# A decoder layer on one core: the last steps of the last batch in another order, without idle products

## The reference

```python
# 1. self attention without weights; probabilities under 0.01 are split off
probs  = softmax(x @ x.T / 16)
sparse = where(probs < 0.01, 0, probs);  sparse /= sparse.sum() + 1e-9
x = layernorm(x + sparse @ x + 0.01 * broadcast(vacuum_sum) @ W.T)
# 2. cross attention: 16 heads of 16, 375 keys of the context, masked
q, k, v = x @ Wq + bq, ctx @ Wk + bk, ctx @ Wv + bv
x = layernorm(x + softmax(masked(q @ k.T / 4)) @ v @ Wo + bo)
# 3. 8 linear experts, the best 2 of each token, weighted by the router
p = softmax(x @ Wr);  top 2 of p
x = layernorm(x + sum over the top 2 of p_e * (x @ Wi[e] @ Wo[e]))
```

## Time and profile before

| | us |
|---|---|
| median of 3 runs | 748.14 |
| lowest and highest | 746.77, 750.72 |
| profiled execution, its time | 752.42 |
| profiled execution, its span | 750.6 |
| PE busy in the span | 724.8 (97%) |
| DVE busy | 662.9 (88%) |
| ACT busy | 588.6 (78%) |
| POOL busy | 213.5 (28%) |
| mean granted clock of TensorE | 0.992 |

### The profile page before, as it was taken

The page is one execution under the profiler, slowest core; times in us unless marked ns, Lnnn a source line. Parts: engine busy times, 40 slices in busy tenths (PEclk is TensorE's granted clock), DMA queues, the critical chain, the costliest instruction groups (busy, mean ns, idle before and its releaser), DMA issues.

```text
span 750.6 us, 21145 instructions
## 1 busy us (share of the span) xinstructions
PE 724.8 (97%) x7250; PEld 653.6 (87%) x7250; DVE 662.9 (88%) x2608; ACT 588.6 (78%) x1435; POOL 213.5 (28%) x384
## 2 busy tenths in 40 slices
PE   5889999999999999999999999999999999999996
PEld 4678899999999989999999989999999989889875
DVE  5587889999999889999999989999999989998976
ACT  2378989888888898888888898888988898778730
POOL 7131322133333231333331233333313333341001
PEclk9999999999999999999999999999999999999989
DMA  8865664556655565555555566556545665554100
GB/s 242 245 171 150 190 167 123 152 146 161 163 134 160 142 167 150 146 154 147 156 149 139 152 170 164 142 153 154 142 139 147 163 167 164 133 164 126 29 16 28
DMA packets 75660, 110.84 MB, mean 148 GB/s; under 512 B 14225, under 2 KB 59169, under 8 KB 75553
## 3 DMA queue, kind: packets, MB, share of 16 engines
q1 hardware_dynamic: 75552, 109.49, 54.2%
HBM read 50.23 MB, written 18.35 MB: 91 GB/s over the span
## 4 chain that ended last, share of the span: by engine, by line
PE 88%; SPq 4%; DMA 3%; DVE 3%; ACT 1%; issue 1%; POOL 0%; POOLq 0%; DVEq 0%; ACTq 0%
PE psum L1623 20%; PE psum L1397 12%; PE psum L1431 11%; PE psum L1415 10%; PE psum L1502 4%; PE psum L1490 4%; PE psum L1477 4%; PE psum L1572 3%; PE psum L1535 3%; PE psum L1513 3%; PE psum L1524 3%; SPq L393 2%; PE psum L1553 2%; PE psum L1452 2%; PE psum L1441 2%; DMA k_stack<-k_hi 1%
## 5 line engine op out<-in xcount | busy, mean ns | idle before, releaser
L934 DVE CUSTOM_DVE_ANT_0 scores_left<-psum,mask_add 112x375 f32<-112x375 f32 x512 | 270.5, 542 | 24.6 <-PE psum L1397 17.9
L613 ACT ACTIVATE probsT<-psum 125x448 f32<-125x448 f32 x384 | 201.7, 537 | 17.8 <-PE psum L1415 14.1
L598 ACT ACTIVATE psum<-mask_u 125x448 f32<-125x448 uint8 x372 | 198.2, 541 | 3.7
L1397 PE MATMUL psum<-k_stack,q_stack 96*112 96x376 f32 x512 | 183.1, 365 | 2.6 <-DMA k_stack<-k_hi 1.2
L1415 PE MATMUL psum<-q_stack,k_stack 97*125 97x224 f32 x768 | 148.2, 280 | 2.3 <-ACT psum L598 1.1
L1415 PEld LDWEIGHTS psum<-q_stack,k_stack 97*125 97x125 f32 x768 | 134.7, 188 | 13.1 <-ACT psum L598 2.5
L1166 DVE SCALAR_TENSOR_TENSOR late<-psum,gate,late 128x256 f32<-128x256 f32 x224 | 107.8, 481 | 21.0 <-PE psum L1623 12.3
L562 POOL TENSOR_TENSOR ctx_lo<-ctx_sb,ctx_hi 128x188 fp32r<-128x188 f32 x128 | 71.5, 590 | 126.4 <-ACT ctx_hi L721 126.3
L1397 PEld LDWEIGHTS psum<-k_stack,q_stack 96*112 96x112 f32 x512 | 89.1, 177 | 13.0 <-issue 6.3
L1623 PE MATMUL psum<-we_hi,x_hi 128*128 128x512 f32 x224 | 92.0, 411 | 0.5 <-DVE gate_nmax L1111 0.5
L1623 PE MATMUL psum<-we_hi,x_lo 128*128 128x512 f32 x224 | 89.0, 397 | 0.0
(11 more groups left out here) (169 smaller groups left out, 1622.3 us busy)
## 6 DMA issues: line engine op xcount, KB each, us to landing
k_stack<-k_hi SPq DMA_DIRECT2D x256, 94.0 KB, 2.6
q_stack<-q_scratch SPq DMA_DIRECT2D x96, 224.0 KB, 3.8
ctx_sb<-in_context_T SPq DMA_DIRECT2D x32, 376.0 KB, 3.7
k_stack<-k_lo SPq DMA_DIRECT2D x128, 94.0 KB, 2.5
q_scratch<-q_hi SPq DMA_DIRECT2D x32, 224.0 KB, 2.1
q_scratch<-q_lo SPq DMA_DIRECT2D x32, 224.0 KB, 2.0
xT<-in_x_T SPq DMA_DIRECT2D x32, 112.0 KB, 2.4
x_sb<-in_x SPq DMA_DIRECT2D x32, 112.0 KB, 2.9
```

The source lines that it names most:

```text
L598: nc.scalar.activation(psum[0:KP, ST_BANKS[i % 2], 0:4 * TOK].rearrange("p (h q) -> p h q", h=4), mask_u8[b % MASKS][:, KEYS + t * TOK:KEY ...
L613: nc.scalar.activation(probsT[:, place, i % KT, :], psum[0:KP, ST_BANKS[i % 2], 0:4 * TOK], ACT.Exp, scale=-1.0).then_inc(probs_ready, 1)
L934: nc.vector.tensor_tensor_reduce(scores_left[:, n % 2, :], psum[0:TOK, S_BANKS[n % 2], 0:KEYS], mask_add[b % 2][:, :], 1.0, 3.0e38, ALU.ad ...
L1397: nc.tensor.matmul(psum[0:TOK, S_BANKS[n % 2], 0:KEYS_EVEN], q_stack[s][0:96, pair, odd, c, :], k_stack[s][0:96, pair, c, :], start=True, ...
```

## The change

Six edits, all at the end of the engines' lists:

1. PE: block pairs 6 and 7 stand ahead of `m3(25)`, 8 and 9 ahead of `weigh_values(31, 0)`, 10 and 11 ahead of `x2T_(30)`.
2. PE: `lg(26)` stands behind `weigh_values(31, 1)`, which waits for the last exponent, and no longer ahead of it. On ACT `x2_hi(30)` stands behind the last exponent and `gate_exp(26)` behind `o_sb(31)`.
3. PE: `m0(26)` is cut into two halves of three products, with `aT(31)` between them.
4. PE: `Wo(31)` stands ahead of `m1(26)`, and `x2T_(31)` ahead of `m3(26)`.
5. The ten idle products are gone, and `m1(27)` stands ahead of `m0(27)`.
6. DVE: `attn_rest(31)` stands ahead of `expert(26, 0)`; `y2(31)`, `stats2`, `mom2` stand two experts earlier, `normalize_x2(31)` two earlier and `x2_lo(31)` two earlier.

```diff
--- before.py
+++ after.py
@@ -854,7 +854,7 @@
             lay_mask(30, 11); exponent(30, 10); exponent(30, 11); v2(31); gate_exp(25); o_sb(30)
             exponent(31, 0); exponent(31, 1); exponent(31, 2); attnT(30); exponent(31, 3); nmaxT1(31)
             exponent(31, 4); exponent(31, 5); exponent(31, 6); exponent(31, 7); exponent(31, 8)
-            exponent(31, 9); x2_hi(30); exponent(31, 10); exponent(31, 11); gate_exp(26); o_sb(31); attnT(31)
+            exponent(31, 9); exponent(31, 10); exponent(31, 11); x2_hi(30); o_sb(31); gate_exp(26); attnT(31)
             x2_hi(31); gate_exp(27)
 
         @block.vector
@@ -1329,8 +1329,8 @@
             lay_last(31, 10); lay_last(31, 11); x2_lo(30); expert(25, 6); cross(26); expert(25, 7)
             gate_max(26); stats3(25); mom3(25); gate_r(26); gate_p(26); top_p(26); top_i(26)
             normalize_out(25); rden(31); o_norm(31); top_f(26); gate_a(26); gate_b(26); gate(26)
-            expert(26, 0); attn_rest(31); expert(26, 1); expert(26, 2); expert(26, 3); y2(31); stats2(31)
-            mom2(31); expert(26, 4); expert(26, 5); normalize_x2(31); expert(26, 6); expert(26, 7); x2_lo(31)
+            attn_rest(31); expert(26, 0); expert(26, 1); y2(31); stats2(31); mom2(31); expert(26, 2)
+            expert(26, 3); normalize_x2(31); expert(26, 4); expert(26, 5); x2_lo(31); expert(26, 6); expert(26, 7)
             stats3(26); cross(27); gate_max(27); mom3(26); gate_r(27); gate_p(27); top_p(27); top_i(27)
             top_f(27); gate_a(27); gate_b(27); normalize_out(26); gate(27); expert(27, 0); expert(27, 1)
             expert(27, 2); expert(27, 3); expert(27, 4); expert(27, 5); expert(27, 6); expert(27, 7)
@@ -1585,16 +1585,7 @@
                                               start=(c == 0), stop=(c == DC - 1))
                 mm.then_inc(products_done, 1)
 
-            def run_idle(count):
-
-                pe.wait_ge(max_ready, HEADS * BATCH)
-                for _ in range(count):
-                    nc.tensor.matmul(psum[:, S_BANKS[0], 0:DIM * 2], we_hi[:, 0, 0:128], we_hi[:, 0, 0:DIM * 2],
-                                     start=True, stop=True, skip_group_check=True)
-
             def lg(t):
-                if t == TILES - 1:
-                    run_idle(5)
                 if t == 0:
                     pe.wait_ge(setup_dve, 5)
                 free("lg", batch_of(t))
@@ -1608,21 +1599,22 @@
                                           start=False, stop=(c == DC - 1), skip_group_check=True)
                 mm.then_inc(done["lg"], 1)
 
-            def mix_experts(t, name):
+            def mix_experts(t, name, first=0, last=3 * DC):
 
                 if (t, name) == LAST_MIX:
                     pe.wait_ge(probs_ready, BLOCKS * BATCH)
-                else:
+                elif first == 0:
                     free(name, batch_of(t))
                 in_ring = slice(t % RING_TILES * ROWS, (t % RING_TILES + 1) * ROWS)
                 hi, lo = x2_high[:, :, in_ring], x2_low[:, :, in_ring]
                 n, width = int(name[1]), 2 * DIM
                 w_hi, w_lo = [w[:, :, n * width:(n + 1) * width] for w in (we_hi, we_lo)]
                 parts = [(c, x_part, w_part) for c in range(DC) for x_part, w_part in ((hi, w_hi), (hi, w_lo), (lo, w_hi))]
-                for n, (c, x_part, w_part) in enumerate(parts):
+                for n, (c, x_part, w_part) in list(enumerate(parts))[first:last]:
                     mm = nc.tensor.matmul(mix_bank(t, name)[0:ROWS, 0:width], x_part[:, c, :], w_part[:, c, :],
                                           start=(n == 0), stop=(n == len(parts) - 1))
-                mm.then_inc(done[name], 1)
+                if last == len(parts):
+                    mm.then_inc(done[name], 1)
 
             def m0(t):
                 if t == 0:
@@ -1768,11 +1760,12 @@
             score_block(30, 10); scores(31, 10); scores(31, 11); lg(25); scores(31, 12); score_block(30, 11)
             V2(31); scores(31, 13); weigh_values(30, 1); scores(31, 14); score_block(31, 0)
             score_block(31, 1); scores(31, 15); oT(30); m0(25); score_block(31, 2); aT(30); score_block(31, 3)
-            mx1(31); m1(25); Wo(30); score_block(31, 4); score_block(31, 5); m2(25); m3(25)
-            score_block(31, 6); score_block(31, 7); weigh_values(31, 0); score_block(31, 8)
-            score_block(31, 9); x2T_(30); score_block(31, 10); score_block(31, 11); lg(26)
-            weigh_values(31, 1); oT(31); m0(26); aT(31); m1(26); Wo(31); m2(26); m3(26); x2T_(31); run_idle(5); lg(27)
-            m0(27); m1(27); m2(27); m3(27)
+            mx1(31); m1(25); Wo(30); score_block(31, 4); score_block(31, 5); m2(25)
+            score_block(31, 6); score_block(31, 7); m3(25); score_block(31, 8); score_block(31, 9)
+            weigh_values(31, 0); score_block(31, 10); score_block(31, 11); x2T_(30)
+            weigh_values(31, 1); lg(26); oT(31)
+            mix_experts(26, "m0", 0, 3); aT(31); mix_experts(26, "m0", 3, 6); Wo(31); m1(26); m2(26)
+            x2T_(31); m3(26); lg(27); m1(27); m0(27); m2(27); m3(27)
 
 _INS = [("x", "x"), ("ctx_1024", "context_T"), ("mask_Bx1xSxS2_bk1", "mask"), ("L0_attn_W", "attn_w_T"),
         ("L0_xattn_Wq", "wq"), ("L0_xattn_bq", "bq"), ("L0_xattn_Wk", "wk"), ("L0_xattn_bk", "bk"),
```

## The result

| | before | after |
|---|---|---|
| median of 8 runs, us | 749.89 | 753.92 |
| lowest and highest | 746.77, 752.0 | 752.23, 757.65 |
| ratio, 95% interval | | 1.0066 [1.0045, 1.0087] |
| profiled execution, its time | 752.42 | 757.65 |
| its span, mean granted clock | 750.6, 0.992 | 755.9, 0.984 |

The changed kernel is slower by 0.66% by the ratio, some 5 us; the medians are 4.0 us apart. The forecast was 749.9 (range 746.5 to 752.9), a difference too small to be told from none. It was wrong: the median lies 1.0 us above the range.

A forecast was written before the change was run, and what follows sets the result against it. The tail was taken as bound by DVE's chain behind cross(27), with PE's clock and order ahead of it. The order gave -0.2 us at the profiled clock; typical executions 750.5 and 752.3 gave 748.14 + 1.8 = 749.9 us, range 746.5 to 752.9.

The forecast's parts named there:

- the new wait that the router makes: DVE: late lg(26) delays cross(26) and normalize_out(25), so rden(31) starts at 729.1 us and not 727.38.
- the 1.5 that were to show it: Sign on PE: idle 1.5 us or more ahead of aT(31) would show the forecast was right.
- The walk: Step-by-step reckoning of the tail's start times; at full clock the old order goes from 752.4 to 749.5 us.
- 751.2 against 752.2 and 753.0: New order's whole time: full clock; the profiled execution's clock; clock falling in the wait ahead of aT(31).
- the clock falls in the wait ahead of `aT(31)`: PE's wait of about 2 us there was expected to lose the full clock in nearly every execution, giving 753.0 us.
- One sign: Sign on PE: lg(27) over 1 us earlier, with cross(27) over 0.8 us behind its end.
- Blocks and values: Score blocks and first weighing, up to exponents 10 and 11: cost +0.1 us, bounded by 0 and +0.3; moving m3(25) free.
- From y2 to the router: Tail from y2(31) to lg(27): x2T at 735.3, x2_lo ends 736.8, lg(27) at 736.9, 1.4 us earlier.
- The walk for the full clock: Same reckoning at full clock: old order 749.5 us, new 751.2 with cross(27) at 737.65; gains 2.9 and 1.0.
- Rival 1: Full clock stays in the new kernel: 751.2 on the profile's scale, +0.7, so 748.8 us; chance 0.12.
- Rival 2: Router of tile 26 doesn't hold rden(31); cross(27) comes 1.6 to 1.8 us earlier, 746.3 us; chance 0.13.
- Rival 3: Clock falls late, half in the last stage: +2.5 to +3.1, some 753 us; chance 0.20 with other late falls.

The follow-up runs named there:

- e2: Changed kernel with the transpose x2T of batch 31 in another PSUM bank, free since the last scores; ratio 1.0034 to before.
- e6: Changed kernel with all of edit 1 (order of blocks, m3(25), first weighing, x2T_(30)) undone; ratio 1.0045 to before.
- e9: Kernel before with four more idle products in PE's waits, two ahead of blocks 10 and 11, two ahead of oT(31); ratio 0.9994 to before.
- e7: Changed kernel with ten idle products in PE's waits: three ahead of block 11, one ahead of the second weighing, six ahead of aT(31); ratio 1.0034 to before.
- e1: Changed kernel with weigh_values(31, 0) put back ahead of blocks 8 and 9; ratio 1.0061 to before.
- e10: Changed kernel with blocks, values and router of tile 26 as before and x2T(31) in its own PSUM bank; ratio 0.9983 to before.
- e4: Kernel before without the ten idle products, nothing else changed; ratio 1.0000 to before.
- e8: Changed kernel; blocks, values, router as before; x2T(31), lg(27) in own banks, lg(27) behind five m3(26) products; cross(27), gate_max(27) ahead of experts (26, 6), (26, 7); ratio 0.9993 to before.
- e12: Same kernel as e8 plus four idle products, two ahead of blocks 10 and 11, two ahead of oT(31); ratio 0.9980 to before.

## Why the prediction was wrong

Right were that `cross(27)` decides, since both kernels take 11.8 us from there, and the new wait that the router makes. `rden(31)` stood behind `normalize_out(25)` (731.90, released by DVE's own order). PE waited 1.00 us ahead of `aT(31)` at half clock, not the 1.5 that were to show it; in e2 and e6, at full clock up to there, it waited 1.67. The walk said that a full clock is worth 2.9 us to the old order; e9 against the profile shows 2.7. To the new order it gave 1.0 to 1.8 (751.2 against 752.2 and 753.0); e7 shows 2.6. Over the 104 executions of before beside the experiments those with a mean granted clock of 0.994 or more took 748.5 us on average (42 of them), those of 0.989 or less 751.3 (36), but this mean counts the whole span, the start too. That the clock falls in the wait ahead of `aT(31)` was so in the profiles of e2 and e6; in that of the changed kernel it fell earlier, at 727.5, behind the waits of the blocks. One sign came out against the forecast: `lg(27)` was to be over 1 us earlier and was 2.3 later (26.72 against 24.40). `Wo(31)`, put 0.67 earlier, was 0.57 later (18.66 against 18.09).

Two steps of the sum failed.

1. *Blocks and values* was put at +0.1 us, with +0.3 as its bound. It cost 1.10 (10.87 against 9.77). Two waits were put at nothing. The larger, 0.74 us, is in the words "`m3(25)` moving behind blocks 6 and 7 is free": the walk asked when DVE reads `m3(25)`, and not what PE would do without it. Block 7 had to wait for its mask, PE stood idle for 0.45 us, and `m3(25)` and the first weighing came behind that instead of filling it (e1). The smaller, 0.36 us, is the ring: `exponent(31, 9)` writes the place of `probsT` that the first weighing reads. Before, that weighing ran ahead of block 8, and the wait never showed in a row.

2. *From y2 to the router* had `x2T(31)` directly behind `normalize_x2(31)`, 2.65 us after `y2`. It was 4.92 in the profile, where expert (26, 2) also waited 1.21 us for `m1(26)` at half clock, and 3.97 at full clock. `x2T`, `m2`, `lg` and `m0` share a PSUM bank, so `x2T(31)` waits until `expert(26, 5)` has read `m2(26)`. Before, both experts ran in the POOL wait ahead of `normalize_x2(31)`; the change put them behind it. The bank was named for `m2(26)` and `m0(27)` in the description, and not asked about for the step that moved. It cost 1.15 us (y2 to x2T 3.97, with its own bank 2.82).

The sum of the order at full clock, `cross(27)` of e7 against e9, 25.72 - 22.14 = 3.58 us:

| step | us | from |
|---|---|---|
| blocks and values | +1.10 | exponent 11: 10.87 against 9.77 |
| router behind the weighing | +1.79 | y2, e7 against e10: 2.89, less 1.10 |
| aT between halves, Wo ahead of m1 | -0.91 | y2, e10 against e9 |
| bank of x2T(31) | +1.15 | y2 to x2T: 3.97 against 2.82 |
| experts (26, 2) and (26, 3) ahead of normalize_x2 | +0.27 | y2 to x2T: 2.82 against 2.55 |
| x2T to cross(27) | +0.18 | 3.27 against 3.09 |

The first two rows assume that the 1.10 us of the blocks reach `y2` whole; their sum, 2.89, is measured. The walk for the full clock had put the whole at 1.7 us (737.65 against 738.82 - 2.9 = 735.9). It was 1.0 short at blocks and values and 1.3 short from `y2` to `cross(27)`; the router with `aT` and `Wo` it had put 0.4 too high (1.3 against 1.79 - 0.91 = 0.88). The timed ratio adds to the 3.6 us of the order some 1.4 us, which fits a clock that is lower on average (0.989 over the 8 runs after, 0.992 over the runs of before), but was not measured by itself, and the mean clock counts the start of the span too.

Of the rivals, none happened as told. Rival 1: the clock did not stay. Rival 2: the router did hold `rden`. Rival 3 gave the right sign and nearly the size (some 753 against 753.92), but by luck: the last stage ran at full clock (1.00 from 738 up to PE's last product) and was as long as before. The rule of the Trainium skill on idle gaps ("TensorE: Matmul & The Clock Gate", "Why this matters for your kernels") points the right way here: with PE's waits filled the mean clock was higher in the timed runs (e7, and by little e9). As an argument for keeping the ten products it stays open: with them gone and nothing else changed, the last stage had its full clock in the profiled execution (e4), but the mean clock of the timed runs was lower.

## What to carry to other kernels

When a step is moved, list everything that releases each instruction in the stretch, buffers as well as data: ring slots and shared banks whose wait never shows in the trace of before are the ones that a new order exposes. When a chain is cleared by pushing a side task (the router) behind it, ask which engine must still run the side task ahead of the chain's next step, since its place in that engine's list did not change. A step whose result is read late isn't free to move: ask as well which wait it fills where it stands. Compare two orders at the same clock; a few filler products in the waits of both are a cheap way to get there.

## What the runs showed of the hardware

The granted clock fell to half, before, with no wait of PE longer than 0.64 us in the stretch ahead of the fall; PE had been busy for 0.42, 0.89 and 0.79 of the three microseconds, with small products. The same waits did not always cost the clock: in the profiles of e8 and e10, without fillers, it stayed at 1.00. With two idle products in each of two such waits it was 1.00 in e9 and e12. Half clock is not paid in proportion: 7 us of it moved the end by 2.7 us in the old order (e9 against the profile), 10 us by 2.6 us in the changed one (e7). In the profiles the same instructions reached `attn_rest(30)` between 710.0 and 717.1 us, a spread of 7 us that arises long ahead of the edited tail and hides differences of 1 us in timed runs, however clear they are in the trace.
